# Groups of two row units instead of four in batches 2 to 6 of a masked graph layer with LayerNorm, with a new start and a new end

## The chip, the cores and the metric
One core of one Trainium2 chip. The metric is the device time of one launch in microseconds (us). The kernel before takes 120.64 us, the median of 3 runs (120.59 to 120.68). PE is TensorE (PEld its weight loads), DVE is VectorE, ACT is ScalarE, POOL is GpSimd, SP is SyncE, which issues the transfers.

## The reference
Eight batches, 1024 nodes of 128 features, four relations with a 128x128 weight each. adj holds 0 or 1 for these inputs, of type int32, so only the mask of relation 1 has ones.

```python
x, adj        # (8, 1024, 128) float32; (8, 1024, 1024) int32
masks = (adj[None] == rel_ids[:, None, None, None]).astype(x.dtype)
h = jnp.einsum('rbnm,bmd->rbnd', masks, x)
y = jnp.einsum('rbnd,rdo->bno', h, weight) + bias
out = layernorm(x + y, axis=-1)            # eps 1e-5
```

## The kernel before, in words
A batch has 1024 rows in eight **units** of 128 rows. Relation 1 alone is computed; meanwhile the kernel checks that adj holds 0 and 1 only and that x is in range, and a second pass for all relations runs if not (here it doesn't).

For each unit:
- SP loads adj, 0.5 MiB a unit; from batch 1's second pair on, two units (a pair, 1 MiB) at a time (`load_adj`, L398). Three slots of a batch each, a ring: a load waits until the pair three batches back is transposed and checked.
- PE transposes the low half-words of the unit, eight 128x128 blocks (`transpose_unit`, L601), into one of four PSUM banks `ids_t`.
- DVE makes bf16 0/1 values of them in `mask_t` (`mask_unit`, L699).
- ACT checks a pair with a squaring activation (`check`, L522).

For each batch, x is split into a float16 high part `x_hi` (ACT, `split_hi`, L531) and the rest `x_lo` (POOL, `split_lo`, L448; DVE in batch 0). POOL then adds the bias to x in place (`add_bias`, L454), for the residual sum.

Rows go on in **groups** of units (`split`, L70): four units in batches 2 to 6, in batch 1 two, in batch 0 one or two, in batch 7 four, two, one, one. For each group PE makes 16 matmuls, eight with x_hi and eight with x_lo, with up to 512 moving columns (`products`, L619), ACT copies the result to SBUF (`copy_h`, L535), PE multiplies it with the weight, one fp32 matmul a unit, into `y_ps` (`project`, L633), DVE adds x plus bias (`sum_rows`, L705), and makes statistics (L711) and moments (L717). For each batch ACT takes a square root (`root`, L539), DVE a reciprocal (`offer_guess`, L727), POOL refines it in seven small operations (`roots`, L465 to L481) and normalises the rows (L488). SP stores them after all loads.

**Order.** Each engine's program is written out by hand. PE's step for group g (L661 to L668) is: for each unit of the next group, transpose it, then do that share of g's products; the projection of group g-1 stands before the last share. So a group of two is: transpose, half the products, transpose, projection of g-1, half the products. `project(g)` for a group before the last four waits for the sum of group g-1 (L631), since both use `y_ps`.

DVE's step for g (L796 to L817): the sum of g-2, masks of the next group's units with the statistics of g-2, the row maxima of x_hi (in a batch's first group) and, where g-2 ends a batch, moments and the reciprocal between them.

ACT's step for g (L558 to L568): copy_h of g-1; where g is the last group of its batch, split_hi of the next batch; then the checks that `pairs_checked_by` gives to g, and after the first of them the root of a batch that g-2 ended.

POOL's order (L494 to L499) is, for each b: split_lo(b+1), roots(b-1), normalise(b-1), add_bias(b+1). `split_lo` waits for `s_hi`, and `sum_rows` (L704) for `s_xb`, which `add_bias` counts up:

```python
for b in range(B - 1):
    split_lo(b + 1)
    if b >= 1:
        roots(sets[b - 1])
        normalise(sets[b - 1], sets[b - 1].units)
    add_bias(b + 1)
```

SP's order: units of batch 0 with the weight behind unit 1, unit (1,0), x(1), unit (1,1), three pairs of batch 1, x(2), then for each batch from 2 its four pairs and the next batch's x. x(0) is loaded whole from ACT's queue. A batch is read with rows p*8+s in batches 0 and 1 and in blocks of two rows (`step`) later.

At the end, batch 7 is normalised in two sets of four units, the first (`ra`) on POOL and ACT, the second (`rb`) with a chain of five small DVE operations after its root.

Of the kernel before, what the change touches and what calls it, by code (L numbers as in the profile page):

```python
# [5 lines left out]
P = 128  # L6
FP32 = mybir.dt.float32
# [4 lines left out]
ALU = mybir.AluOpType  # L12
# [27 lines left out]
def adj_resnorm_kernel(nc, x, adj, weight, bias, out):  # L40
# [14 lines left out]
    def step(b):  # L55
        return J if b < EARLY else 2

# [12 lines left out]
    def split(b):  # L70
        if b == 0:
            return [(0, 1), (1, 1), (2, 2), (4, 2), (6, 2)]
        if b == 1:
            return [(0, 2), (2, 2), (4, 2), (6, 2)]
        return [(0, 4), (4, 2), (6, 1), (7, 1)] if b == B - 1 else [(0, 4), (4, 4)]

# [33 lines left out]
    def pairs_checked_by(g):  # L110

        first = [1, 2, 2, 3, 4, 5, 6, 7, 8, 11, 13]
        if g.index < len(first):
            return first[g.index]
        return min(PAIRS * (g.b + 1) + (2 if ends_batch(g) else 0), PAIRS * B)

    ctx = ExitStack()
    with ctx:
# [8 lines left out]

        ident = sb("ident", [P, P], BF16)
        ones = sb("ones", [P, 1], FP32)
        row_of_ones = sb("row_of_ones", [1, P], FP32)  # L130
# [53 lines left out]
        s_biased = sem("bias_ready")  # L184
        s_unit = [[sem(f"unit_loaded{b}{u}") if alone(b, u) else None for u in range(J)] for b in range(EARLY)]
        s_x = [sem(f"x_loaded{b}") for b in range(B)]
        s_adj = [[sem(f"adj_loaded{slot}{k}") for k in range(PAIRS)] for slot in range(ADJ_SLOTS)]
# [3 lines left out]
        s_zero = sem("ident_zeroed")  # L191
        s_ident = sem("ident_ready")
        s_const = sem("constants_ready")
        s_still = sem("zeros_ready")
# [196 lines left out]
        def _(sp):  # L391
# [17 lines left out]

            load_unit(0, 0)  # L410
            load_unit(0, 1)
            sp.dma_start(w_sb[:, 0, :], weight[0]).then_inc(s_w, 16)  # L412
            for u in range(2, J):
                load_unit(0, u)
            load_unit(1, 0)
            load_x(1)
            load_unit(1, 1)
            for k in range(1, PAIRS):
                load_adj(1, k)
            load_x(2)  # L420
            for b in range(EARLY, B):
                for k in range(PAIRS):
                    load_adj(b, k)
                if b + 1 < B:
                    load_x(b + 1)

# [11 lines left out]
        def _(pool):  # L438
            nc.gpsimd.memset(ident[:, :], 0.0).then_inc(s_zero, 1)
            pool.wait_ge(s_zero, 1)  # L440
            nc.gpsimd.affine_select(out=ident[:, :], in_=ident[:, :], compare_op=ALU.not_equal, fill=1.0,
                                    base=0, pattern=[[-1, P]], channel_multiplier=1).then_inc(s_ident, 1)

            def split_lo(b):
# [56 lines left out]
            roots(full)  # L501
            normalise(full, full.units[:4])
            roots(ra)
# [5 lines left out]
        def _(act):  # L509
# [15 lines left out]

            def split_hi(b, js, signal):
                act.wait_ge(s_x[b], 16)
                if b >= 2:
                    act.wait_ge(s_prod, last_group_of(b - 2) + 1)
                    act.wait_ge(s_rm, b - 1)  # L530
                nc.scalar.activation(x_hi[:, b % 2, js], x_sb[:, b, js], ACT.Copy).then_inc(signal, 1)  # L531
# [16 lines left out]

            act.dma_start(units_of(x_sb[:, 0], 0, 0, J), rows_of(x, 0, 0, J)).then_inc(s_x[0], 16)
            act.dma_start(bias_row[:, :], bias.rearrange("(a d) -> a d", a=1)).then_inc(s_bias, 16)  # L550
            act.preload_act_table(ACT.Sqrt)
            split_hi(0, slice(0, HALF), s_hi0)
            split_hi(0, slice(HALF, J), s_hi)
            act.wait_ge(s_spread, 1)
# [3 lines left out]
            for g in groups[1:LAST]:  # L558
                b = g.b
                copy_h(groups[g.index - 1])  # L560
                if ends_batch(g):
                    split_hi(b + 1, slice(0, J), s_hi)
                todo = range(pairs_checked_by(groups[g.index - 1]), pairs_checked_by(g))
                for n, at in enumerate(todo):
                    check(at // PAIRS, at % PAIRS)
                    q = groups[g.index - 2] if g.index >= 2 else None
                    if n == 0 and q and ends_batch(q):
                        root(sets[q.b])  # L568
            a, c, e, d = groups[LAST:]
# [6 lines left out]
            copy_h(c)  # L576
            normalise(full, full.units[4:5])
            copy_h(e)
            root(ra)
            normalise(full, full.units[5:7])  # L580
            copy_h(d)
            normalise(full, full.units[7:]).then_inc(s_aside, 1)
            root(rb)
# [5 lines left out]
        def _(pe):  # L589
# [35 lines left out]
            def project(g):  # L625
# [6 lines left out]
                for n in range(g.count):  # L632
                    last = nc.tensor.matmul(y_of(g)[:, n, :], h_all[:, g.bank, n * P:(n + 1) * P], w_sb[:, 0, :],  # L633
                                            start=True, stop=True)
                last.then_inc(s_y, 1)

            def idle_turns(n):
# [4 lines left out]
            pe.wait_ge(s_still, 1)  # L642
            idle_turns(9)
            pe.wait_ge(s_ident, 1)
# [8 lines left out]
            transpose_unit(0, 1)  # L653
            products(g, 1, 2)
            g = groups[1]
            products(g, 0, 2)
            transpose_unit(0, 2)
            project(groups[0])
            products(g, 1, 2)
            transpose_unit(0, 3)  # L660
            for g in groups[2:LAST + 1]:  # L661
                coming = coming_after(g)
                for n, u in enumerate(coming):
                    transpose_unit(groups[g.index + 1].b, u)

                    if n == (len(coming) - 1 if g.index < LAST else 1):
# [8 lines left out]
            products(d, 0, 1)  # L675
            project(e)
            pe.wait_ge(s_found, 1)
            nc.tensor.matmul(ids_t[0][0:1, 0, 0:2].bitcast(FP32), found[:, :], ones[:, :],
                             start=True, stop=True).then_inc(s_count, 1)
            project(d)  # L680
            second_pass(pe, second_pe)

        @block.vector
        def _(dve):
# [23 lines left out]
            def statistics(g):  # L708
                dve.wait_ge(s_sum, g.index + 1)
                for u in g.units:  # L710
                    last = nc.vector.bn_stats(stats[:, u, :], rows[:, g.b, u, :])  # L711
                last.then_inc(s_st, 1)

            def combine(r, g, units):
# [38 lines left out]

            def normalise(r, units):
                wait_for_rstd(dve, r)
                slot = r.b
                for u in units:
                    last = nc.vector.tensor_scalar(rows[:, slot, u, :], rows[:, slot, u, :], mean[:, slot, u:u + 1],  # L758
                                                   rstd[:, slot, u:u + 1], ALU.subtract, ALU.mult)
                last.then_inc(s_done, 1)  # L760

# [79 lines left out]
            combine(rb, c, c.units)  # L841
            for g in (e, d):
                sum_rows(g)
                statistics(g)
            combine(rb, d, range(J - 2, J))
            dve.wait_ge(s_count, 1)
            nc.vector.tensor_copy(again[:, :], ids_t[0][0:1, 0, 0:2].bitcast(FP32)).then_inc(s_again, 1)
            for part in (invert, times_guess, times_guess_again, better_guess, shift_rows):
                part(rb)
            normalise(rb, rb.units[2:])  # L850
            second_pass(dve, second_dve)
# [17 lines left out]
```

## Time and profile before
| | |
|---|---|
| median of 3 runs | 120.64 us |
| the profiled execution | 120.54 us |
| its span | 118.8 us |
| PE busy | 106.6 us, 90% |
| DVE, ACT, POOL busy | 84.8 (71%), 88.1 (74%), 70.3 us (59%) |
| transfers | 42.22 MB, mean 355 GB/s |
| granted clock of PE | 0.985 |

The span is the time from the first to the last instruction in the trace; the execution's own time is 1.74 us longer. Times in rows are counted from the start of the span. The timeline's rows give start, length, engine, line, operation, tiles and count, and in brackets how long the engine was idle before and what ended that. Runs of equal instructions are merged into a row, and its length ends with the last of them; matmuls overlap, so the distance of two starts says more than a length.

### The profile page before, as it was taken

To read this page: it belongs to the slowest core of one execution; us is meant where nothing else is said; L and a number is where in the kernel's file an instruction comes from. 1 tells how busy PE (TensorE), PEld (TensorE's weight loads), DVE (VectorE), ACT (ScalarE), POOL (GpSimd) and SP (SyncE) were. 2 spreads that over 40 slices of the span, in tenths; PEclk is the share of its full clock that TensorE was granted. 3 is DMA by queue.
4 is the path that set the end of the run, shared out by engine and by line. 5 is a ranking of instruction groups with operands and counts; after the bars stand their busy time and mean duration, and the time that the engine had idled before them with its cause. 6 is when DMAs were issued, how large, how long until landed. Compare 5 with 4: busy or idle time off the path is not lost.

```text
span 118.8 us, 2879 instructions
## 1 busy us (share of the span) xinstructions
PE 106.6 (90%) x1012; PEld 80.4 (68%) x1023; DVE 84.8 (71%) x252; ACT 88.1 (74%) x114; POOL 70.3 (59%) x132
## 2 busy tenths in 40 slices
PE   6788999899999979999999999999999999999400
PEld 2168898799997646767676767676868676679300
DVE  1055678397877848696959887787779777998840
ACT  4088277947797999799999499968987698925530
POOL 2007001940047998399569955995689577977740
PEclk9999999999999999999999999999999999999985
DMA  3999999999999999999999999999999999450271
GB/s 73 389 408 411 414 407 422 414 391 412 425 414 384 419 403 436 380 414 414 419 391 404 422 406 394 420 406 423 377 433 411 415 399 383 141 177 0 85 248 35
DMA packets 12419, 42.22 MB, mean 355 GB/s; under 512 B 882, under 2 KB 7155, under 8 KB 8947
## 3 DMA queue, kind: packets, MB, share of 16 engines
q1 hardware_dynamic: 12256, 41.49, 88.6%
q10 hardware_dynamic: 146, 0.52, 1.3%
q8 instruction: 9, 0.15, 0.5%
q14 instruction: 8, 0.06, 0.1%
HBM read 37.81 MB, written 4.19 MB: 354 GB/s over the span
## 4 chain that ended last, share of the span: by engine, by line
PE 58%; DMA 29%; SPq 5%; DVE 2%; issue 1%; ACT 0%; DVEq 0%
PE h_ps L619 32%; DMA adj_sb<-adj 29%; PE ids_t L601 16%; PE y_ps L633 9%; SPq L396 4%; PE ids_t L633 1%; DVE x_sb L758 0%; SPq L393 0%; SPq L412 0%; ACT std L539 0%; DVE stats L711 0%; DVE x_sb L705 0%; DVE moments L717 0%; DVEq L255 0%; DVE shift L751 0%
## 5 line engine op out<-in xcount | busy, mean ns | idle before, releaser
L522 ACT ACTIVATE junk<-adj_sb,minus 128x2048 bf16<-128x2048 int32 x32 | 63.8, 1994 | 0.4 <-DMA adj_sb<-adj 0.4
L699 DVE TENSOR_SCALAR mask_t<-ids_t 128x1024 bf16<-128x1024 uint16 x64 | 43.6, 687 | 25.2 <-PE ids_t L601 24.1
L601 PEld LDWEIGHTS ids_t<-ident,adj_sb 128*128 128x128 bf16 x512 | 36.5, 123 | 13.8 <-DMA adj_sb<-adj 2.7
L601 PE MATMUL ids_t<-ident,adj_sb 128*128 128x128 bf16 x512 | 40.0, 221 | 2.3 <-DMA adj_sb<-adj 2.2
L619 PE MATMUL h_ps<-mask_t,x_lo 128*128 128x512 bf16 (+2 forms) x184 | 33.5, 314 | 0.0
L619 PE MATMUL h_ps<-mask_t,x_hi 128*128 128x512 bf16 (+2 forms) x173 | 31.1, 310 | 1.2 <-DVE mask_t L699 0.6
L448 POOL TENSOR_TENSOR x_lo<-x_sb,x_hi 128x1024 f16<-128x1024 f32 x7 | 15.0, 2144 | 24.2 <-ACT x_hi L531 24.2
L488 POOL TENSOR_SCALAR x_sb<-x_sb,rstd,shift 128x128 f32<-128x128 f32 x55 | 24.0, 457 | 1.0
L535 ACT ACTIVATE h_all<-h_ps 128x512 f32<-128x512 f32 (+2 forms) x23 | 10.6, 463 | 18.1 <-PE h_ps L619 18.1
L454 POOL TENSOR_TENSOR x_sb<-x_sb,bias_sb 128x1024 f32<-128x1024 f32 x8 | 19.0, 2377 | 7.8 <-DVE x_lo L764 7.7
L619 PEld LDWEIGHTS h_ps<-mask_t,x_hi 128*128 128x128 f16 x184 | 15.6, 98 | 7.2 <-DVE mask_t L699 1.2
L619 PEld LDWEIGHTS h_ps<-mask_t,x_lo 128*128 128x128 f16 x184 | 16.4, 98 | 5.9
L633 PE MATMUL y_ps<-w_sb,h_all 128*128 128x128 f32 x120 | 17.8, 284 | 0.0
L633 PEld LDWEIGHTS y_ps<-w_sb,h_all 128*128 128x128 f32 x120 | 15.0, 192 | 0.1
L711 DVE BATCH_NORM_STATS2 stats<-x_sb 128x6 f32<-128x128 f32 x64 | 14.5, 280 | 0.1
L705 DVE TENSOR_TENSOR x_sb<-y_ps,x_sb 128x512 f32<-128x512 f32 (+2 forms) x20 | 11.0, 552 | 1.9 <-PE y_ps L633 1.0
L531 ACT ACTIVATE x_hi<-x_sb 128x1024 f16<-128x1024 f32 (+1 forms) x9 | 8.5, 954 | 3.1 <-DMA x_sb<-x 3.1
L692 DVE TENSOR_REDUCE row_max<-x_hi 128x8 f32<-128x1024 f16 x8 | 9.6, 1202 | 0.0
L522 ACT ACTIVATION_READ_ACCUMULATOR junk<-adj_sb,minus 128x1 f32 x32 | 6.1, 190 | 0.0
L640 PE MATMUL h_ps<-mask_t 128*128 128x512 bf16 x11 | 4.6, 586 | 1.2 <-DVE mask_t L787 1.2
L717 DVE BATCH_NORM_AGGREGATE moments<-stats 128x2 f32<-128x6 f32 x64 | 5.3, 154 | 0.1
L470 POOL TENSOR_TENSOR product<-sixteenth,first_guess 128x8 f32<-128x8 f32 (+1 forms) x8 | 1.6, 203 | 6.2 <-DVE first_guess L727 6.0
(44 smaller groups left out, 30.8 us busy)
## 6 DMA issues: line engine op xcount, KB each, us to landing
adj_sb<-adj SPq DMA_DIRECT2D x27, 1024.0 KB, 19.5
adj_sb<-adj SPq DMA_DIRECT2D x10, 512.0 KB, 8.4
x_sb<-x SPq DMA_DIRECT2D x7, 512.0 KB, 18.9
out<-x_sb SPq DMA_DIRECT2D x7, 512.0 KB, 16.7
x_sb<-x ACTq DMA_DIRECT2D x1, 512.0 KB, 5.4
out<-x_sb SPq DMA_DIRECT2D x2, 256.0 KB, 3.3
w_sb<-weight SPq DMA_DIRECT2D x1, 64.0 KB, 6.1
bias_row<-bias ACTq DMA_DIRECT2D x1, 0.5 KB
```

What stands on the lines that cost most here:

```text
L448: nc.gpsimd.tensor_tensor(x_lo[:, b % 2], x_sb[:, b], x_hi[:, b % 2], ALU.subtract).then_inc(s_lo, 1)
L454: nc.gpsimd.tensor_tensor(x_sb[:, b], x_sb[:, b], bias_sb[:, :].unsqueeze(1).to_broadcast([P, J, D]), ALU.add).then_inc(s_xb, 1)
L488: last = nc.gpsimd.tensor_scalar(rows[:, slot, u, :], rows[:, slot, u, :], rstd[:, slot, u:u + 1], shift[:, slot, u:u + 1], ALU.mult, ALU.add)
L522: nc.scalar.activation(junk[:, at % 2], adj_sb[:, slot, 2 * k:2 * k + 2, :], ACT.Square, scale=2.0, bias=minus[:, 0:1], accum_out=squares[ ...
L535: nc.scalar.activation(h_all[:, g.bank, 0:g.count * P], h_ps[g.bank][:, 0:g.count * P], ACT.Copy).then_inc(s_h, 1)
L601: last = nc.tensor.transpose(bank[:, j, :], words[:, j // step(b), j % step(b), 0, :], ident[:, :])
L619: last = nc.tensor.matmul(h_ps[g.bank][:, 0:g.count * P], part[:, g.b % 2, j, :], mask_t[:, g.b % 2, j, g.cols], start=(j == 0 and part is ...
L633: last = nc.tensor.matmul(y_of(g)[:, n, :], h_all[:, g.bank, n * P:(n + 1) * P], w_sb[:, 0, :], start=True, stop=True)
L692: nc.vector.tensor_reduce(row_max[:, b, :], x_hi[:, b % 2], AX.X, ALU.max, apply_absolute_value=True).then_inc(s_rm, 1)
L699: nc.vector.tensor_scalar(mask_t[:, b % 2, :, u * P:(u + 1) * P], ids_t[u % T_BANKS][:, :, :].bitcast(UINT16), 1.0, None, ALU.mult).then_i ...
L705: nc.vector.tensor_tensor(rows[:, g.b, g.us, :], y_of(g)[:, 0:g.count, :], x_sb[:, g.b, g.us, :], ALU.add).then_inc(s_sum, 1)
L711: last = nc.vector.bn_stats(stats[:, u, :], rows[:, g.b, u, :])
```

## The change
- `split`: batches 2 to 6 in groups of two units, as batch 1 already; `step` is 2 in batch 1 too.
- x(0) is loaded in halves on SP behind unit (0,0); each half has a semaphore for its split. x(1) goes behind unit (1,1), and from batch 2 on x(b) behind the second pair of its own batch.
- In batch 0, PE transposes units 2 and 3 a step earlier; one idle matmul less ahead.
- ACT does split_hi(b+1) after the first check of the step instead of ahead of the checks; `pairs_checked_by` spreads the checks one or two to a group.
- The last unit (group d): PE adds x into y with an fp32 identity (`add_x`), DVE takes statistics and normalises from PSUM, no sum_rows; the count's matmul goes behind. ACT's and POOL's shares of batch 6's normalisation are 2 units on POOL and 6 on ACT instead of 4 and 4.

```diff
-        return J if b < EARLY else 2
+        return J if b == 0 else 2
...
-        if b == 1:
-            return [(0, 2), (2, 2), (4, 2), (6, 2)]
-        return [(0, 4), (4, 2), (6, 1), (7, 1)] if b == B - 1 else [(0, 4), (4, 4)]
+        return [(0, 4), (4, 2), (6, 1), (7, 1)] if b == B - 1 else [(0, 2), (2, 2), (4, 2), (6, 2)]
...
-        first = [1, 2, 2, 3, 4, 5, 6, 7, 8, 11, 13]
+        first = [1, 2, 2, 3, 4, 5, 6, 7, 8, 10, 11]
...
-        return min(PAIRS * (g.b + 1) + (2 if ends_batch(g) else 0), PAIRS * B)
+        return min(PAIRS * g.b + g.place + (2 if g.b < 4 else 3), PAIRS * B) if g.b < B - 1 else PAIRS * B
...
             load_unit(0, 0)
+            for n in range(2):
+                sp.dma_start(x_sb[:, 0, n * HALF:(n + 1) * HALF, :], rows_of(x, 0, n * HALF, HALF)).then_inc(s_x0[n], 16)
             load_unit(0, 1)
...
             load_unit(1, 0)
+            load_unit(1, 1)
             load_x(1)
-            load_unit(1, 1)
             for k in range(1, PAIRS):
                 load_adj(1, k)
-            load_x(2)
-            for b in range(EARLY, B):
+
+            for b in range(2, B):
                 for k in range(PAIRS):
                     load_adj(b, k)
-                if b + 1 < B:
-                    load_x(b + 1)
+                    if k == 1:
+                        load_x(b)
...
+            pool.wait_ge(s_ident, 1)
+            nc.gpsimd.tensor_copy(whole_ident[:, :], ident[:, :]).then_inc(s_whole, 1)
...
-            normalise(full, full.units[:4])
+            normalise(full, full.units[:2])
...
                 copy_h(groups[g.index - 1])
-                if ends_batch(g):
-                    split_hi(b + 1, slice(0, J), s_hi)
                 todo = range(pairs_checked_by(groups[g.index - 1]), pairs_checked_by(g))
                 for n, at in enumerate(todo):
                     check(at // PAIRS, at % PAIRS)
-                    q = groups[g.index - 2] if g.index >= 2 else None
-                    if n == 0 and q and ends_batch(q):
-                        root(sets[q.b])
+                    if n == 0:
+                        q = groups[g.index - 2] if g.index >= 2 else None
+                        if q and ends_batch(q):
+                            root(sets[q.b])
+                        if ends_batch(g):
+                            split_hi(b + 1, slice(0, J), s_x[b + 1], s_hi)
...
-            normalise(full, full.units[4:5])
+            normalise(full, full.units[2:3])
             copy_h(e)
             root(ra)
-            normalise(full, full.units[5:7])
+            normalise(full, full.units[3:5])
             copy_h(d)
-            normalise(full, full.units[7:]).then_inc(s_aside, 1)
+            normalise(full, full.units[5:]).then_inc(s_aside, 1)
...
+            def add_x(g):
+
+                pe.wait_ge(s_whole, 1)
+                pe.wait_ge(s_xb, g.b + 1)
+                nc.tensor.matmul(y_of(g)[:, 0, :], whole_ident[:, :], x_sb[:, g.b, g.first, :], start=True, stop=False)
...
-            idle_turns(9)
+            idle_turns(8)
...
             products(g, 1, 2)
+            transpose_unit(0, 2)
             g = groups[1]
             products(g, 0, 2)
-            transpose_unit(0, 2)
+            transpose_unit(0, 3)
             project(groups[0])
             products(g, 1, 2)
-            transpose_unit(0, 3)
...
             project(e)
+            add_x(d)
+            project(d)
...
-            project(d)
...
-            for g in (e, d):
-                sum_rows(g)
-                statistics(g)
+            sum_rows(e)
+            statistics(e)
+            statistics_of_sum(d)
```

## Rows read from the trace of the kernel before

**Rows 1.** The page, engine busy time, share of the span, instructions
```profile
PE 106.6 (90%) x1012; PEld 80.4 (68%) x1023; DVE 84.8 (71%) x252; ACT 88.1 (74%) x114; POOL 70.3 (59%) x132
```

**Rows 2.** Windows, one batch: stretch, length, busy of PE, PEld, DVE, ACT, POOL, clock, DMA share, GB/s
```profile
55.68:68.05 12.37, 12.27 (x111) 8.70 (x112) 9.96 (x29) 10.77 (x14) 9.43 (x18) 1.00 1.03 410
```

**Rows 3.** Timeline, transposes on PE that waited for a load of adj
```profile
6.42 0.70 PE L601 MATMUL ids_t<-ident,adj_sb 128*128 128x128 bf16 x8 [1.21 <-DMA adj_sb<-adj]
...
22.84 0.73 PE L601 MATMUL ids_t<-ident,adj_sb 128*128 128x128 bf16 x8 [0.42 <-DMA adj_sb<-adj]
...
43.30 0.64 PE L601 MATMUL ids_t<-ident,adj_sb 128*128 128x128 bf16 x8 [0.58 <-DMA adj_sb<-adj]
```

**Rows 4.** Timeline, PE, batch 3: a group of four between its first transposes
```profile
49.52 0.61 PE L601 MATMUL ids_t<-ident,adj_sb 128*128 128x128 bf16 x8
...
54.84 1.03 PE L619 MATMUL h_ps<-mask_t,x_lo 128*128 128x512 bf16 x4
...
55.71 0.61 PE L601 MATMUL ids_t<-ident,adj_sb 128*128 128x128 bf16 x8
```

**Rows 5.** Timeline, PE, batch 1: groups of two
```profile
26.15 0.67 PE L601 MATMUL ids_t<-ident,adj_sb 128*128 128x128 bf16 x8
...
27.53 0.66 PE L601 MATMUL ids_t<-ident,adj_sb 128*128 128x128 bf16 x8
...
28.03 0.66 PE L633 MATMUL y_ps<-w_sb,h_all 128*128 128x128 f32 x4
...
28.53 1.04 PE L619 MATMUL h_ps<-mask_t,x_lo 128*128 128x256 bf16 x8
...
29.41 0.67 PE L601 MATMUL ids_t<-ident,adj_sb 128*128 128x128 bf16 x8
...
32.65 0.61 PE L601 MATMUL ids_t<-ident,adj_sb 128*128 128x128 bf16 x8
```

**Rows 6.** Timeline, POOL and DVE: a sum of two units, add_bias(3), and batch 3's first sum
```profile
26.32 0.42 DVE L705 TENSOR_TENSOR x_sb<-y_ps,x_sb 128x256 f32<-128x256 f32 x1
...
53.77 2.37 POOL L454 TENSOR_TENSOR x_sb<-x_sb,bias_sb 128x1024 f32<-128x1024 f32 x1
...
61.23 0.69 DVE L705 TENSOR_TENSOR x_sb<-y_ps,x_sb 128x512 f32<-128x512 f32 x1
```

**Rows 7.** Timeline, ACT, the last step of batch 1 and a check after it
```profile
32.85 0.38 ACT L535 ACTIVATE h_all<-h_ps 128x256 f32<-128x256 f32 x1 [0.79 <-PE h_ps L619]
...
33.13 1.05 ACT L531 ACTIVATE x_hi<-x_sb 128x1024 f16<-128x1024 f32 x1
...
37.17 1.99 ACT L522 ACTIVATE junk<-adj_sb,minus 128x2048 bf16<-128x2048 int32 x1
```

**Rows 8.** Timeline, POOL: split_lo(2), the first of roots(0), normalise(0), add_bias(2)
```profile
34.26 2.14 POOL L448 TENSOR_TENSOR x_lo<-x_sb,x_hi 128x1024 f16<-128x1024 f32 x1 [9.30 <-ACT x_hi L531]
36.49 0.20 POOL L465 TENSOR_SCALAR sixteenth<-moments 128x8 f32<-128x8 f32 x1
...
38.60 3.47 POOL L488 TENSOR_SCALAR x_sb<-x_sb,rstd,shift 128x128 f32<-128x128 f32 x8
42.02 2.38 POOL L454 TENSOR_TENSOR x_sb<-x_sb,bias_sb 128x1024 f32<-128x1024 f32 x1
```

**Rows 9.** Timeline, the end: PE's long step of batch 7, sum of its first group, last root
```profile
99.01 0.61 PE L601 MATMUL ids_t<-ident,adj_sb 128*128 128x128 bf16 x8
...
107.25 0.69 DVE L705 TENSOR_TENSOR x_sb<-y_ps,x_sb 128x512 f32<-128x512 f32 x1
...
112.20 0.30 ACT L539 ACTIVATE std<-moments,eps 128x4 f32<-128x4 f32 x1 [1.14 <-DVE moments L717]
```

**Rows 10.** Windows after the last matmul, columns as in rows 2
```profile
114.20:114.80 0.60, 0.00 (x0) 0.00 (x0) 0.02 (x1) 0.00 (x0) 0.00 (x0) 1.00 0.60 201
114.80:115.40 0.60, 0.00 (x0) 0.00 (x0) 0.00 (x0) 0.00 (x0) 0.00 (x0) 0.77 0.98 309
```

More of the change, by code:

```diff
@@ L128, in adj_resnorm_kernel @@
         ident = sb("ident", [P, P], BF16)
+        whole_ident = sb("whole_ident", [P, P], FP32)
         ones = sb("ones", [P, 1], FP32)
@@ L185, in adj_resnorm_kernel @@
         s_unit = [[sem(f"unit_loaded{b}{u}") if alone(b, u) else None for u in range(J)] for b in range(EARLY)]
+        s_x0 = [sem(f"half_of_first_x_loaded{n}") for n in range(2)]
         s_x = [sem(f"x_loaded{b}") for b in range(B)]
@@ L192, in adj_resnorm_kernel @@
         s_ident = sem("ident_ready")
+        s_whole = sem("whole_ident_ready")
         s_const = sem("constants_ready")
@@ L524, in check, with split_hi @@
                                      accum_out=squares[:, at:at + 1]).then_inc(s_check, 1)
-            def split_hi(b, js, signal):
-                act.wait_ge(s_x[b], 16)
+            def split_hi(b, js, loaded, signal):
+                act.wait_ge(loaded, 16)
                 if b >= 2:
@@ L547, in normalise @@
                 return last
-            act.dma_start(units_of(x_sb[:, 0], 0, 0, J), rows_of(x, 0, 0, J)).then_inc(s_x[0], 16)
             act.dma_start(bias_row[:, :], bias.rearrange("(a d) -> a d", a=1)).then_inc(s_bias, 16)
             act.preload_act_table(ACT.Sqrt)
-            split_hi(0, slice(0, HALF), s_hi0)
-            split_hi(0, slice(HALF, J), s_hi)
+            split_hi(0, slice(0, HALF), s_x0[0], s_hi0)
+            split_hi(0, slice(HALF, J), s_x0[1], s_hi)
             act.wait_ge(s_spread, 1)
@@ L633, in project @@
                     last = nc.tensor.matmul(y_of(g)[:, n, :], h_all[:, g.bank, n * P:(n + 1) * P], w_sb[:, 0, :],
-                                            start=True, stop=True)
+                                            start=g.index < len(groups) - 1, stop=True)
                 last.then_inc(s_y, 1)
+            def add_x(g):
+                pe.wait_ge(s_whole, 1)
+                pe.wait_ge(s_xb, g.b + 1)
+                nc.tensor.matmul(y_of(g)[:, 0, :], whole_ident[:, :], x_sb[:, g.b, g.first, :], start=True, stop=False)
             def idle_turns(n):
@@ L712, in statistics, with statistics_of_sum @@
                 last.then_inc(s_st, 1)
+            def statistics_of_sum(g):
+                dve.wait_ge(s_y, g.index + 1)
+                nc.vector.bn_stats(stats[:, g.first, :], y_of(g)[:, 0, :]).then_inc(s_st, 1)
             def combine(r, g, units):
@@ L752, in shift_rows, with normalise @@
                                                in1=rstd[:, r.b, r.us], op0=ALU.mult, op1=ALU.mult).then_inc(s_rstd_last, 1)
-            def normalise(r, units):
+            def normalise(r, u, source):
                 wait_for_rstd(dve, r)
[L756 to L760, printed above, removed]
+                return nc.vector.tensor_scalar(rows[:, r.b, u, :], source, mean[:, r.b, u:u + 1], rstd[:, r.b, u:u + 1],
+                                               ALU.subtract, ALU.mult)
             def split_lo(b, js, hi, lo):
@@ L849, in _ @@
                 part(rb)
-            normalise(rb, rb.units[2:])
+            normalise(rb, e.first, rows[:, rb.b, e.first, :])
+            normalise(rb, d.first, y_of(d)[:, 0, :]).then_inc(s_done, 1)
             second_pass(dve, second_dve)
```

## The prediction, made before the change was run
> **What bounds the kernel now.** I read the page's busy shares first: TensorE is busy 106.6 of 118.8 us [rows 1]. A share can hide stages, so the windows came next: a whole batch in the middle takes 12.37 us and TensorE is busy 12.27 of it, at granted clock 1.00, while VectorE has 9.96, ScalarE 10.77, GpSimd 9.43 [rows 2]. The transfers move 410 GB/s there, so one MiB takes 2.56 us and a batch's 4.5 MiB 11.5 us: close behind, but not the bound. The chain of waits in order of time shows where that was otherwise: TensorE waited for a pair of adj at 22.84 and at 43.30, and before its first transpose at 6.42 [rows 3]; from 43.30 to 111.24 it has no gap. The two waits lie 8 MiB of queue apart (7 MiB up to pair (1,1), 15 up to pair (3,0)): 8 x 2.56 = 20.5 us, as observed. So there are two clocks: the transfers until 43, TensorE afterwards.
>
> **The start.** The first x no longer shares the start with unit 0, so unit 0 has 0.5 MiB less in front of it: first transpose 1.28 us earlier, near 5.1 instead of 6.42 [rows 3]. Transposing a unit ahead takes away mask waits of 0.3 us or so. But pair (1,1) stands behind the same 7 MiB as before, so TensorE only waits longer at 22.84: I count 0. The two half loads and the later ones are issued on SP 0.4 us apiece, faster than they move; bounds of the start: 1.3 gained, 0.5 lost. x(1), now behind unit (1,1), lands 1 MiB before pair (1,1), at 22.84 - 2.56 = 20.3; the products want its split half a microsecond after 22.84. From batch 2 on, x comes after the second pair: x(2) lands 3.5 MiB ahead of the old place of (3,0), at 43.3 - 9.0 = 34.3, and its split starts at 35.1 (below): no cost. It is also moved past the slot waits of two pairs on SP, which end a batch or more before need. The fp32 identity is one small GpSimd copy in its idle time at the start: 0. One idle matmul fewer: 0.
>
> **Groups of two: TensorE.** A group of four takes 49.52 to 55.71 = 6.19 us [rows 4]. Batch 1 already has groups of two: 26.15, 29.41, 32.65, so 3.25 each, 6.50 for four units [rows 5]. The products themselves cost the same: four of 512 columns 0.87 (54.84 to 55.71), eight of 256 columns 0.88 (28.53 to 29.41). What is added is one more switch between transposes, products and projection for every four units. That is 0.31 us per four units, 0.62 per batch, 3.1 us for the five batches 2 to 6. The Trainium skill (TensorE: Matmul & The Clock Gate, LDWEIGHTS) prices a weight load at its columns over 1.2 GHz, 107 ns for 128, and twice as many loads are issued; by it a matmul of 256 columns is only just covered. The rows agree that it is still covered, at 110 ns each.
>
> **Groups of two: the wait that appears.** Three edits meet. (a) split_hi(b+1) stands in the last step of batch b, which was half a batch (6.19 us) and is now a quarter (3.25), and it now stands behind a check of 1.99 us. (b) GpSimd's order is unchanged: split_lo(b+1), roots(b-1), normalise(b-1), add_bias(b+1). (c) sum_rows of the first group of batch b needs add_bias(b). It comes two steps later: that was the start of the next batch, and is now the middle of the same one. Before, add_bias(3) was over at 53.77 + 2.37 = 56.14 and sum_rows wanted it at 61.23: 5.1 us of slack [rows 6]. Now, from the start c of the last step of a batch:
> - ScalarE: copy_h starts at c + 0.20 (32.65 to 32.85), 0.28 to the next instruction, the check 1.99, split_hi 1.05 [rows 5, 7]: c + 3.52.
> - GpSimd: 0.08 handover, then split_lo at 34.26 to the end of add_bias at 42.02 + 2.38 = 44.40, 10.14 us without a gap [rows 8]: c + 13.74.
> - VectorE: handover 0.05 (an estimate from the 0.08 just shown), sum_rows of two units 0.42 [rows 6]: c + 14.21. Here project of the second group waits, since it may not write y_ps before this sum.
> - TensorE: handover and first weight load 0.12, project 0.50, half the products 0.87: c + 15.7. That is the last step of the next batch, which starts the ring again.
>
> So a batch takes **15.7 us**, and not 4 x 3.25 = 13.0: TensorE is ready for that projection two and a half steps into the batch and a bit, at c + 3 x 3.25 + 0.50 + 0.88 + 0.45 = 11.6, so it stands for 2.6 us. (x_lo is ready at c + 5.75, where TensorE wants it at c + 3.25 + 2.3 = 5.55: a wait of 0.2 that this stall swallows.) VectorE's masks are queued behind the waiting sum_rows: two masks (0.69 each) and 0.48 of statistics after it end at c + 16.1, when the first half products of the last step want them: just in time. Nothing else is late, for VectorE's 9.96 and ScalarE's 10.77 us per batch [rows 2] grow by under 1 us each (two more sums of 0.42 and two more copies, for halves of the old ones), in a batch of 15.7, and GpSimd has 10.1. No engine is full; it is a ring of dependences.
>
> **The sum.** The last step of batch 1 starts at 32.65 as before. Five turns of the ring (add_bias 2 to 6): 32.65 + 5 x 15.7 = 111.15. That step now transposes four units for batch 7, two more than 3.25 us hold: 4.1 us, so batch 7's own long step begins at 115.25. It began at 99.01 [rows 9]: **+16.24**. In batch 7 add_bias(7) ends 13.74 - 4.1 = 9.64 after that start, and sum_rows of its first group wanted it after 107.25 - 99.01 = 8.24. The root of batch 6 follows it on GpSimd (2.1 us, 36.49 to 38.60), so shift(6) comes at 11.7 instead of 9.6. ScalarE's copy of group e is queued behind a normalise that waits for it: 0.49, then copy 0.26, root 0.30, two units 0.86, copy 0.27, three units 1.3, so root(rb) starts at 15.3 instead of 112.20 - 99.01 = 13.19: **+2.1**. The sum for the last unit moves to TensorE (a matmul of 0.25 instead of 0.30 on VectorE), hidden behind this. Everything after root(rb), stores included, is 6.6 us as before; the three last stores come closer together, 0 to 0.3. Span 118.8 + 16.24 + 2.1 = 137.1; the profiled execution lies 1.74 above its span: 138.9. It is 120.54 against a median of 120.64, so add 0.1: **139.0 us**, 15% slower.
>
> Unknown: the five turns at 0.15 each way (0.8), the tail between 0 and 3, the start -1.3 to +0.5, handovers under load. Together 135.6 to 141.8.
>
> **Rivals.**
> 1. The ring does not close: add_bias is early enough, and TensorE alone sets the time. For it: no engine is full, and no stall of this sort is in the trace. Against it: GpSimd's order and 10.14 us [rows 8] against a need at c + 11.6. Then 120.6 + 3.1, less 0.3 in the tail: 123.4. Chance 0.05.
> 2. The stalls lower TensorE's clock. After its last matmul at 111.24 the clock is still 1.00 through 114.80 and falls after it [rows 10], so 3.56 us of idleness were granted and mine are 2.5. It decides from a stall above that; with the next step (3.25 us of work) at half rate each time, 5 x 3.25 = 16 us more: 155. The Trainium skill (TensorE: Matmul & The Clock Gate, The HAM clock gate) states that 1.2 GHz is the idle state and that activity releases 2.4. The rows agree in kind and let this stall pass. Chance 0.04.
> 3. The other side, faster: the first transpose near 5.1 carries through because pair (1,1) lands earlier too, once x does not run on a second queue beside it. This needs the wait of 0.42 at 22.84 [rows 3] not to grow, and both the ring and the 3.1 us of rows 5 to be absent. It gives 120.6 - 1.3 - 0.3 = 119.0. It decides if a two-unit step in mid kernel takes 3.1 and not 3.25 us. Chance 0.03.
>
> **How the numbers follow.** The ring has 0.88, and its range 135.6 to 141.8 holds nine tenths of that: 8 in 10, so the range need not reach the rivals. About 0.2% is what a measurement tells from no change. Faster 0.03 (rival 3), same 0.01 (rivals 1 and 3 blended), slower 0.96.
>
> **What would show it.** In the profile after: the distance between two add_bias instructions in batches 3 to 6 is 15.7 us, GpSimd idle 5.5 us in each, ahead of split_lo; TensorE idle about 2.5 us before a projection in the third step of each batch; VectorE's sum_rows ended by "POOL x_sb L454"-like waits, once per batch; the clock stays 1.00; the wait at 22.84 has grown to about 1.5 us. It is wrong if GpSimd's spacing is 13, if the stall sits before split_lo or a mask, or if the clock drops.

## The result and the profile after

| | before | after |
|---|---|---|
| median | 120.66 us (4 runs) | 142.58 us (4 runs: 141.88, 142.45, 142.71, 144.2) |
| ratio of the times, 95% interval | | 1.181 (1.175 to 1.187) |
| the profiled execution, its span | 120.54, 118.8 us | 141.88, 140.1 us |
| PE busy | 106.6 us, 90% | 114.1 us, 81% |
| granted clock of PE | 0.985 | 0.948 |

The change costs 22 us. The forecast was 139.0, with a range up to 141.8: right in sign and in most of its size (18 of 22 us), and too low. The profiled execution is the fastest of the four. The ratios, here and below, leave out executions more than 1.5% above the fastest of the same kernel: the one of 144.2 us here, one each in E1, E4 and E5, two in E9, and one of 623.75 us of the kernel before beside E1 to E4, which stays unexplained.

The page of the changed kernel, busy time and the chain that ended last:

```profile
PE 114.1 (81%) x1183; PEld 100.1 (71%) x1184; DVE 87.7 (63%) x261; ACT 89.7 (64%) x126; POOL 69.8 (50%) x131
...
POOL 45%; issue 33%; PE 6%; DMA 5%; ACT 4%; SPq 2%; DVE 1%; DVEq 0%; POOLq 0%
```

Against [rows 1] the other engines have about the work they had, and all have a smaller share of a longer span. TensorE shows 7.5 us more. E3 below does the same work without stalls and has 107.9 us, so some 6 us of these are matmuls at a lower clock. The chain now runs through GpSimd, which is busy half the time. That is what a ring of waits looks like: the chain is on an engine with no lack of time.

The waits of the changed kernel (who waited for whom; us in total, times, longest):

```profile
POOL x_lo L453 <- ACT x_hi L536: 52.8, 7, 12.1
...
DVE x_sb L717 <- POOL x_sb L459: 15.2, 5, 3.4
...
PE y_ps L638 <- DVE x_sb L717: 11.9, 5, 2.7
...
PE h_ps L624 <- POOL x_lo L453: 0.6, 3, 0.2
```

Five times, once for each of batches 2 to 6, sum_rows waits for add_bias and a projection for sum_rows. Neither wait was in the trace before. The other wait foreseen, for x_lo, is 0.2 us.

GpSimd's timeline: split_lo and add_bias of batches 2 to 7, in brackets its idle time before:

```profile
37.06 2.15 POOL L453 TENSOR_TENSOR x_lo<-x_sb,x_hi 128x1024 f16<-128x1024 f32 x1 [9.81 <-ACT x_hi L536]
44.85 2.35 POOL L459 TENSOR_TENSOR x_sb<-x_sb,bias_sb 128x1024 f32<-128x1024 f32 x1
52.85 2.15 POOL L453 TENSOR_TENSOR x_lo<-x_sb,x_hi 128x1024 f16<-128x1024 f32 x1 [5.66 <-ACT x_hi L536]
60.62 2.34 POOL L459 TENSOR_TENSOR x_sb<-x_sb,bias_sb 128x1024 f32<-128x1024 f32 x1
69.46 2.15 POOL L453 TENSOR_TENSOR x_lo<-x_sb,x_hi 128x1024 f16<-128x1024 f32 x1 [6.50 <-ACT x_hi L536]
...
85.69 2.14 POOL L453 TENSOR_TENSOR x_lo<-x_sb,x_hi 128x1024 f16<-128x1024 f32 x1 [6.10 <-ACT x_hi L536]
...
101.47 2.15 POOL L453 TENSOR_TENSOR x_lo<-x_sb,x_hi 128x1024 f16<-128x1024 f32 x1 [5.66 <-ACT x_hi L536]
...
118.59 2.15 POOL L453 TENSOR_TENSOR x_lo<-x_sb,x_hi 128x1024 f16<-128x1024 f32 x1 [7.01 <-ACT x_hi L536]
```

From one split_lo to the next: 15.79, 16.61, 16.23, 15.78 and 17.12 us. Two turns are the 15.7 of the forecast within 0.1; three are 0.5 to 1.4 longer. GpSimd's own part, split_lo to the end of add_bias, is 52.85 to 62.96 = 10.11 us, as in [rows 8].

One turn as TensorE and VectorE have it, from the stall of batch 3 on:

```profile
63.06 0.42 DVE L717 TENSOR_TENSOR x_sb<-y_ps,x_sb 128x256 f32<-128x256 f32 x1 [3.33 <-POOL x_sb L459]
...
63.63 0.69 PE L638 MATMUL y_ps<-w_sb,h_all 128*128 128x128 f32 x4 [2.62 <-DVE x_sb L717]
...
64.15 1.88 PE L624 MATMUL h_ps<-mask_t,x_lo 128*128 128x256 bf16 x8
...
65.83 1.06 PE L606 MATMUL ids_t<-ident,adj_sb 128*128 128x128 bf16 x8
...
80.27 0.68 PE L638 MATMUL y_ps<-w_sb,h_all 128*128 128x128 f32 x4 [2.22 <-DVE x_sb L717]
...
82.06 1.06 PE L606 MATMUL ids_t<-ident,adj_sb 128*128 128x128 bf16 x8
...
96.48 0.68 PE L638 MATMUL y_ps<-w_sb,h_all 128*128 128x128 f32 x4 [1.81 <-DVE x_sb L717]
...
112.26 1.20 PE L638 MATMUL y_ps<-w_sb,h_all 128*128 128x128 f32 x4 [2.63 <-DVE x_sb L717]
...
114.95 0.82 PE L606 MATMUL ids_t<-ident,adj_sb 128*128 128x128 bf16 x8
```

(the projections at 80.27, 96.48 and 112.26 are those after the stalls of batches 4, 5 and 6; the transposes at 65.83, 82.06 and 114.95 begin the batch's last step), and the windows over two such stalls, at 46 and at 62 us (stretch, length, busy of PE, PEld, DVE, ACT, POOL, granted clock, DMA share, GB/s):

```profile
46.00:47.00 1.00, 0.00 (x0) 0.00 (x0) 0.00 (x0) 0.00 (x0) 1.00 (x1) 1.00 1.04 421
...
47.80:48.80 1.00, 0.93 (x8) 0.92 (x9) 1.00 (x4) 0.00 (x0) 0.00 (x0) 1.00 1.02 426
...
62.40:63.60 1.20, 0.00 (x0) 0.00 (x0) 0.54 (x2) 0.00 (x0) 0.56 (x1) 1.00 1.00 416
...
64.20:65.00 0.80, 0.80 (x7) 0.55 (x5) 0.80 (x4) 0.00 (x0) 0.00 (x0) 0.50 1.11 461
...
67.00:68.00 1.00, 1.00 (x8) 0.78 (x7) 1.00 (x3) 1.00 (x1) 0.00 (x0) 0.71 1.18 415
```

After the stall at 46 (idle for 2.66 us) the clock stays at 1.00. After that at 62 (idle for 2.62) it is at 0.50, 1.2 instead of 2.4 GHz, from about 64.2 to 67.4. It falls again after the third and the fifth stall. The half of the group's products between the projection and the next last step takes 65.83 - 64.15 = 1.68 us instead of 0.87.

### The profile page after: what moved, and what is told of

The parts are those of the page before. It is cut to its first block, busy times and chain, and to the rows that moved or that the text cites. A ratio compares the mean times of both kernels' runs of the same rounds, so it can differ in the third digit from the quotient of the medians.

```text
span 140.1 us, 3262 instructions
## 1 busy us (share of the span) xinstructions
PE 114.1 (81%) x1183; PEld 100.1 (71%) x1184; DVE 87.7 (63%) x261; ACT 89.7 (64%) x126; POOL 69.8 (50%) x131
## 4 chain that ended last, share of the span: by engine, by line
POOL 45%; issue 33%; PE 6%; DMA 5%; ACT 4%; SPq 2%; DVE 1%; DVEq 0%; POOLq 0%
POOL x_sb L493 15%; POOL x_sb L459 12%; POOL x_lo L453 11%; DMA adj_sb<-adj 5%; PE h_ps L624 3%; PE ids_t L606 2%; ACT junk L527 1%; POOL product L481 1%; POOL minus_mean L472 1%; POOL better L478 1%; POOL rstd L483 1%; POOL product L475 1%; SPq L397 1%; POOL shift L486 1%; POOL sixteenth L470 1%
## 5 line engine op out<-in xcount | busy, mean ns | idle before, releaser
L606 PE MATMUL ids_t<-ident,adj_sb 128*128 128x128 bf16 x512 | 41.2, 225 | 3.5 <-DMA adj_sb<-adj 3.4
L624 PE MATMUL h_ps<-mask_t,x_lo 128*128 128x256 bf16 (+2 forms) x264 | 35.9, 280 | 0.6 <-POOL x_lo L453 0.6
L624 PE MATMUL h_ps<-mask_t,x_hi 128*128 128x256 bf16 (+2 forms) x263 | 34.8, 276 | 0.1
L540 ACT ACTIVATE h_all<-h_ps 128x256 f32<-128x256 f32 (+2 forms) x33 | 12.2, 369 | 33.8 <-PE h_ps L624 33.8
L638 PE MATMUL y_ps<-w_sb,h_all 128*128 128x128 f32 x120 | 20.6, 295 | 11.9 <-DVE x_sb L717 11.9
L624 PEld LDWEIGHTS h_ps<-mask_t,x_lo 128*128 128x128 f16 x264 | 25.3, 102 | 4.6 <-POOL x_lo L453 1.2
L624 PEld LDWEIGHTS h_ps<-mask_t,x_hi 128*128 128x128 f16 x264 | 24.2, 101 | 3.4 <-DVE mask_t L711 0.3
L638 PEld LDWEIGHTS y_ps<-w_sb,h_all 128*128 128x128 f32 x120 | 16.2, 196 | 12.7 <-issue 12.6
L493 POOL TENSOR_SCALAR x_sb<-x_sb,rstd,shift 128x128 f32<-128x128 f32 x53 | 23.2, 454 | 1.2 <-DVE shift L768 0.4
L717 DVE TENSOR_TENSOR x_sb<-y_ps,x_sb 128x256 f32<-128x256 f32 (+2 forms) x30 | 12.5, 416 | 15.2 <-POOL x_sb L459 15.2
L550 ACT ACTIVATE x_sb<-x_sb,shift,rstd 128x128 f32<-128x128 f32 x9 | 4.0, 485 | 2.8 <-POOL shift L486 2.6
```

The source lines that it names most:

```text
L493: last = nc.gpsimd.tensor_scalar(rows[:, slot, u, :], rows[:, slot, u, :], rstd[:, slot, u:u + 1], shift[:, slot, u:u + 1], ALU.mult, ALU.add)
L540: nc.scalar.activation(h_all[:, g.bank, 0:g.count * P], h_ps[g.bank][:, 0:g.count * P], ACT.Copy).then_inc(s_h, 1)
L606: last = nc.tensor.transpose(bank[:, j, :], words[:, j // step(b), j % step(b), 0, :], ident[:, :])
L624: last = nc.tensor.matmul(h_ps[g.bank][:, 0:g.count * P], part[:, g.b % 2, j, :], mask_t[:, g.b % 2, j, g.cols], start=(j == 0 and part is ...
L717: nc.vector.tensor_tensor(rows[:, g.b, g.us, :], y_of(g)[:, 0:g.count, :], x_sb[:, g.b, g.us, :], ALU.add).then_inc(s_sum, 1)
```

## The experiments

Eleven kernels ran, each beside the kernel before on its own chip; the ratios are to that. E1 to E4 shared one chip, E5 to E8 another, E9 to E11 a third.

### E1 to E3: is it the ring?

E1 moves add_bias, E2 moves split_hi, E3 does both.

```diff
                 split_lo(b + 1)
+                add_bias(b + 1)
                 if b >= 1:
                     roots(sets[b - 1])
                     normalise(sets[b - 1], sets[b - 1].units)
-                add_bias(b + 1)
```

```diff
                 copy_h(groups[g.index - 1])
+                if ends_batch(g):
+                    split_hi(b + 1, slice(0, J), s_x[b + 1], s_hi)
...
-                        if ends_batch(g):
-                            split_hi(b + 1, slice(0, J), s_x[b + 1], s_hi)
```

> The changed kernel, but GpSimd does add_bias(b+1) directly behind split_lo(b+1), ahead of roots and normalise. Ring theory (the wait for add_bias makes the stall and so the time): the stall before the projection in the third step disappears in all five batches, add_bias ends 8.1 us after the last step's start where 11.6 is wanted, the distance between two split_lo falls from 15.8 to 17.1 down to about 13.0 us (x_lo may still be 0.4 late), the clock stays 1.00, time 125 to 126.5 us. Rival, that groups of two cost this by themselves (VectorE's masks or the handovers on TensorE): time stays over 138.

> The changed kernel, but split_hi(b+1) stands ahead of the check again. Ring theory: the ring is shorter by exactly the check, 1.99 us, so 13.8 us between two add_bias, stall 0.6 to 1.1 us a batch, too short for the clock to fall: 129 to 130 us. Rival, that the place of split_hi does not matter since ScalarE has spare time: 142 as the changed kernel.

> Both edits: add_bias behind split_lo, split_hi ahead of the check. Ring theory: no ring and no wait for x_lo left, TensorE alone, 4 x 3.14 = 12.56 us a batch, 121 to 122.5 us, about 1 us slower than the kernel before. If something else of groups of two binds (VectorE's row maxima before a mask, copies on ScalarE), the batch takes longer than 12.6 and the windows show which engine TensorE waits for.

| | median us | ratio (interval) | expected |
|---|---|---|---|
| E1 | 125.54 | 1.040 (1.035 to 1.045) | 125 to 126.5 |
| E2 | 129.01 | 1.070 (1.066 to 1.074) | 129 to 130 |
| E3 | 122.80 | 1.018 (1.013 to 1.023) | 121 to 122.5 |

GpSimd of E1, two split_lo in a row, and TensorE's wait between:

```profile
63.19 2.14 POOL L453 TENSOR_TENSOR x_lo<-x_sb,x_hi 128x1024 f16<-128x1024 f32 x1 [2.75 <-ACT x_hi L536]
...
76.14 2.14 POOL L453 TENSOR_TENSOR x_lo<-x_sb,x_hi 128x1024 f16<-128x1024 f32 x1 [2.75 <-ACT x_hi L536]
```

```profile
65.38 1.05 PE L624 MATMUL h_ps<-mask_t,x_lo 128*128 128x256 bf16 x8 [0.20 <-POOL x_lo L453]
```

E2, the same, with the stall that is left:

```profile
63.66 2.15 POOL L453 TENSOR_TENSOR x_lo<-x_sb,x_hi 128x1024 f16<-128x1024 f32 x1 [3.67 <-ACT x_hi L536]
...
77.44 2.15 POOL L453 TENSOR_TENSOR x_lo<-x_sb,x_hi 128x1024 f16<-128x1024 f32 x1 [3.67 <-ACT x_hi L536]
```

```profile
74.44 0.68 PE L638 MATMUL y_ps<-w_sb,h_all 128*128 128x128 f32 x4 [0.96 <-DVE x_sb L717]
```

A batch takes 12.95 us in E1 and 13.78 in E2. The undisturbed turn was 15.79, and the check that E2 takes out of the ring is 1.99 long: 15.79 - 1.99 = 13.80. So the ring has the members and the length that the forecast gave it. The order of two instructions on GpSimd, whose total work is the same, is worth 17 us of the change's 22 (142.58 to 125.54), the falls of the clock among them. E3 leaves no wait on TensorE inside batches 3 to 6; its batches take 12.6 us, and it is 0.3 us above its bracket. Two waits for ScalarE's copies are left in batch 2 (0.31 and 0.89 us).

### E4: the clock

```diff
                 elif g.index <= LAST:
+                    if g.place == 1 and 2 <= g.b < B - 1:
+                        for _ in range(40):
+                            nc.tensor.matmul(spare, ident[:, :], ident[:, :], start=True, stop=True)
                     pe.wait_ge(s_sum, g.index)
```

> The changed kernel with 40 unneeded matmuls of 128 columns (2.2 us) on TensorE in front of the wait for sum_rows, in the third step of batches 2 to 6; they compute nothing that is used. Clock theory (three of the five stalls let the clock fall to half, and this costs the turns their 0.9, 0.5 and 1.4 us over 15.7): all five turns take 15.7 to 15.8 us, clock 1.00 throughout, time 138.8 to 139.4. Rival, that the longer turns have another cause: turns still 16.2 to 17.1, time 141.9 or more.

139.36 us, ratio 1.150 (1.143 to 1.156); the stall in which TensorE idles shrinks to 0.3 us, and the clock is 1.00 in every window of 2 us from 2 to 132 us. One of the five stalls, and its split_lo:

```profile
63.57 0.71 PE L642 MATMUL y_ps<-w_sb,h_all 128*128 128x128 f32 x4 [0.28 <-DVE x_sb L721]
```

```profile
52.91 2.14 POOL L454 TENSOR_TENSOR x_lo<-x_sb,x_hi 128x1024 f16<-128x1024 f32 x1 [5.59 <-ACT x_hi L537]
...
68.59 2.14 POOL L454 TENSOR_TENSOR x_lo<-x_sb,x_hi 128x1024 f16<-128x1024 f32 x1 [5.60 <-ACT x_hi L537]
...
84.26 2.15 POOL L454 TENSOR_TENSOR x_lo<-x_sb,x_hi 128x1024 f16<-128x1024 f32 x1 [5.60 <-ACT x_hi L537]
```

Each of the five turns is 15.7 us now (15.71, 15.68, 15.67, 15.68, 15.69). Work that nobody uses, put into the stall, makes the kernel 3.2 us faster. So the longer turns were the clock's doing, and without them the kernel takes 139.4, the forecast's 139.0 within 0.4. The turns are right by their mechanism; that the total comes so close is also luck, for the start is late by about as much as the end is short (0.8 and 1.0 us in the changed kernel, in the sum further down).

### E5 and E6: the late start

Both are E3 with x(0) in one piece, E5 on ScalarE's queue as in the kernel before, E6 on SP's queue.

E6:

```diff
-            for n in range(2):
-                sp.dma_start(x_sb[:, 0, n * HALF:(n + 1) * HALF, :], rows_of(x, 0, n * HALF, HALF)).then_inc(s_x0[n], 16)
+            load_x(0)
```

E5 has the first line's loop taken out and instead, ahead of the bias on ScalarE's queue:

```diff
+            act.dma_start(units_of(x_sb[:, 0], 0, 0, J), rows_of(x, 0, 0, J)).then_inc(s_x[0], 16)
```

> The kernel with both edits (add_bias behind split_lo, split_hi ahead of the check) and x(0) loaded whole on ScalarE's queue as in the kernel before, not in halves on SP. In the changed kernel the transfers run at some 330 GB/s from 3.5 to 8 us where the kernel before has 410, and pair (1,1) arrives at 24.02 and not 22.84. Theory A (one queue alone, or the halves, slow the start): pair (1,1) is back near 22.8, and the time falls by 0.8 to 1.2 us against the run with both edits (122.8), to 121.6 to 122.0. Rival B (the lateness has to do with x(1), the rows' layout of batch 1 or chance): no change, 122.8.

> As the last, but x(0) whole on SP's queue behind unit (0,0): rows of 4 KB a partition instead of two transfers of 2 KB rows. If the size of the halves is what slows the start, pair (1,1) is back near 22.8 and the time is that of x on ScalarE's queue, 121.6 to 122.0. If it is the single queue, pair (1,1) still arrives near 24 and the time stays 122.8.

E5 122.28 us, 1.011 (1.007 to 1.015), 0.3 above what theory A gave it; E6 123.04 us, 1.019 (1.016 to 1.022), near the 122.8 that was expected if the single queue is the cause. The rates say one thing and the times another. GB/s of the stretches 4 to 5, 5 to 6, 6 to 8 us, from the windows:

| x(0) | run | GB/s |
|---|---|---|
| halves on SP | changed kernel | 328, 324, 346 |
| halves on SP | E3 | 326, 356, 384 |
| whole on SP | E6 | 426, 422, 404 |
| whole on ScalarE's | E5 | 410, 418, 412 |

The halves slow the transfers of the first 8 us, and not the queue: E6 has the changed kernel's queue and the full rate. But pair (1,1) comes at 23.70 in E3, 23.00 in E6 and 24.06 in E5 (from an execution of 123.58 us, well above its median), and the times do not follow the rates. E6 has the full rate and is no faster than E3 (1.019 against 1.018). E5 differs from E6 only by the queue and is 0.8 us faster, with intervals that do not touch. By the times it would be the queue, by the rates the halves, and these runs do not settle it. Over all thirteen traces pair (1,1) comes at 23.5 to 24.2 with the halves (six runs), at 23.0 to 24.1 with x(0) whole and batch 1 in blocks of two rows (E5, E6, E8, E9), and at 22.8 to 23.2 with x(0) whole and rows p*8+s (the kernel before, E10, E11). So the halves are not the only part of the change that goes with a later pair; the layout of batch 1 is another.

### E7 to E9: the rest of the change, with groups of four

E7 is the changed kernel with the groups and checks as before; E8 has x(0) whole on ScalarE's queue too; E9 also has split_hi ahead of the check (the diff of E2) and nine idle matmuls.

```diff
-        return [(0, 4), (4, 2), (6, 1), (7, 1)] if b == B - 1 else [(0, 2), (2, 2), (4, 2), (6, 2)]
+        if b == 1:
+            return [(0, 2), (2, 2), (4, 2), (6, 2)]
+        return [(0, 4), (4, 2), (6, 1), (7, 1)] if b == B - 1 else [(0, 4), (4, 4)]
```

> The changed kernel with groups of four in batches 2 to 6 and the checks spread as in the kernel before; start, order of the loads, end and the place of split_hi behind the check are those of the change. Ring theory: the ring has over 4 us of slack with groups of four, so no stall before a projection and no fall of the clock; TensorE is late by up to 0.9 us at 43 because the transfers start late, and gains 0.3 at the end: 120.0 to 121.3. Rival, that the other edits (split_hi behind a check, start, end) carry a good part of the loss by themselves: over 123.

> As the last, with x(0) whole on ScalarE's queue. If theory A holds, the start is no longer late, and what is left of the change is a gain: 119.4 to 120.4, below the kernel before (120.7). If B holds, equal to the last.

> Groups of four, x(0) whole on ScalarE's queue, split_hi ahead of the check, nine idle matmuls again; the rest as the change has it. In e8 root(rb) starts 13.57 us after the long step of batch 7 begins, and 13.19 in the kernel before, since GpSimd's work begins a check later and shift(6) with it. If that is what eats the new end, it falls to 12.9 or less and the time to 119.9 to 120.5, 0.5 below e8 and faster than the kernel before. If the new end is worth nothing by itself, it stays at e8's 121.0.

E7 121.55 us, 1.008 (1.005 to 1.011); E8 121.03, 1.002 (0.999 to 1.005); E9 120.81, 0.999 (0.996 to 1.002). So everything in the change but the groups costs about 1 us together, with the same late split_hi: the slack of four units swallows it. E7 lies 0.25 above its bracket, E8 0.6 and E9 0.3. E9 was expected 0.5 below E8 and is 0.2 below in the median, well within the intervals. It is not shown that its edits make the kernel faster. E7 and E8 have the new wait of the end, ScalarE's normalise for shift(6). E7's ACT:

```profile
109.87 0.49 ACT L552 ACTIVATE x_sb<-x_sb,shift,rstd 128x128 f32<-128x128 f32 x1 [1.15 <-POOL shift L488]
```

and behind it the copy of group e, for which TensorE then waits. In the kernel before this wait was 0.17 us, and in E9 it is 0.16.

### E10 and E11: batch 1's row layout

E10 is E5, and E11 is E9, with one line undone:

```diff
-        return J if b == 0 else 2
+        return J if b < EARLY else 2
```

> e5 (groups of two, both edits, x(0) whole on ScalarE's queue) with the row layout of batch 1 as in the kernel before (rows p*8+s instead of blocks of two rows). Theory C: a transpose whose stationary operand is read with a stride of 32 bytes takes longer than one with 8, eight transposes 0.50 us and not 0.45, so the steps of batch 1 go from 3.14 back to 3.25 us; and x(1) in rows of 1 KB is what makes the transfers dip to 370 GB/s from 14 to 18 us, so the dip goes. Time within 0.4 of e5 (122.3), since the two offset. If the steps stay at 3.14, the layout has no part in it.

> e9 with batch 1's row layout as in the kernel before. By theory C 0.1 us a step lost in batch 1, hidden in the wait for transfers at 37 to 43 us, and the dip at 14 to 18 us gone: equal to e9 within 0.4.

E10 122.50 us, 1.013 (1.009 to 1.017), as expected. E11 **120.39 us, 0.9955 (0.9936 to 0.9974)**: the one version whose interval lies below the kernel before, by half a per cent. It still holds several edits of the change, and no run separates which of them gives this. Batch 1's steps on TensorE in the changed kernel and in E10:

```profile
27.18 0.61 PE L606 MATMUL ids_t<-ident,adj_sb 128*128 128x128 bf16 x8
...
30.32 0.61 PE L606 MATMUL ids_t<-ident,adj_sb 128*128 128x128 bf16 x8
```

```profile
26.46 0.67 PE L605 MATMUL ids_t<-ident,adj_sb 128*128 128x128 bf16 x8
...
29.71 0.67 PE L605 MATMUL ids_t<-ident,adj_sb 128*128 128x128 bf16 x8
```

3.14 us with blocks of two rows, 3.25 with rows p*8+s. The steps bear out theory C, and so do the rates: the transfers from 14 to 18 us run at 369, 372 and 382 GB/s in E5, E6 and E8, and at 415 in E10 and 410 in E11. The changed kernel itself, whose start was slow already, has 408 there, so this part is shown for the runs with x(0) in one piece alone. E11's median is 0.4 below E9's on the same chip, at the edge of what was expected, and their intervals overlap.

E11 also shows what the new end can give. Its long step of batch 7 and its last root:

```profile
98.49 0.61 PE L607 MATMUL ids_t<-ident,adj_sb 128*128 128x128 bf16 x8
...
111.36 0.30 ACT L544 ACTIVATE std<-moments,eps 128x4 f32<-128x4 f32 x1
```

12.87 us apart, the 12.9 expected of E9 (which has 12.86), against 13.57 in E8 and 13.19 in [rows 9]. With split_hi early, GpSimd reaches shift(6) early, and the end is 0.3 us shorter; with split_hi late, it is 0.4 longer.

## Where the prediction was right, and where it fell short

By its own steps, for the profiled execution:

- **The bound before, the cost of 256 columns, the ring.** Right, and by the mechanism that was forecast: GpSimd idle 5.66 to 7.01 us ahead of split_lo, TensorE idle 1.81 to 2.66 us before the projection in each third step. From c = 49.26 the split_lo starts at c + 3.59 (3.60 forecast), add_bias ends at c + 13.70 (13.74), and sum_rows at 63.48, c + 14.22 (14.21). E1, E2 and E4 took the ring apart term by term.
- **"So 3.56 us of idleness were granted and mine are 2.5", rival 2 at 0.04.** This step failed, and it is why the time left the range: "the clock stays 1.00" was counted on, and a clock that drops was among the forecast's own signs of being wrong. It took one stretch of idleness, at the end of the kernel before, for a bound that stalls elsewhere must reach. Stalls of 2.62, 2.22 and 2.63 us were followed by a clock of 1.2 GHz, those of 2.66 and 1.81 were not. It also priced the fall as a whole step at half rate each time, 16 us. Only what is on the ring counts: the projection and half the products. In turn two 65.83 - 64.15 = 1.68 us instead of 0.87, hence 0.8; in turn three (80.27 to 82.06) 1.79 instead of 1.39, hence 0.4; in turn five (112.26 to 114.95) 2.69 instead of 1.39, hence 1.3. Together 2.5 of the 3.0 us by which the five turns, 81.5 us, exceed 78.5; the rest is 0.1 us a turn. It was a part of the forecast's own case and not a rival to it: here the falls came behind the ring's stalls. The fall varies from run to run: the four runs have a mean clock of 0.948 (141.88 us), 0.924 (142.45), 0.926 (142.71) and 0.919 (144.2). Only the first has a trace, so that the other three are longer for the same reason is likely and not shown.
- **"I count 0" for the start.** The first transpose came at 5.09, as forecast (5.1). Pair (1,1) came at 24.02 and not 22.84: 1.2 us lost where the bound was 0.5. In the first 10 us the transfers moved 266 GB/s in the mean instead of 304, 0.38 MB less, which at 410 GB/s is 0.9 of the 1.2 us. The step set x(0)'s 0.5 MiB as bytes in a queue and took the rate for the same whatever the size of the rows.
- **Groups of two at 3.25 us, 3.1 us in all.** Oversized. The 3.25 was read from batch 1, whose layout the change alters too; the new step takes 3.14, so with no ring the cost is 12.6 - 12.38 = 0.2 us a batch. The step blamed one more switch for all of the 0.31 us per four units; 0.22 of it was the row layout, and 0.09 is left for the switch. [rows 5] show it already: eight transposes of batch 1 take 0.67 us, those at 32.65, which are of batch 2, 0.61. In the ring the term has no weight, and in batch 1 the new layout gave 0.4 us back before the ring begins. It is also the sign that rival 3 named, a step of 3.1 us, and rival 3 did not hold: the ring was there and the wait for pair (1,1) grew.
- **The tail.** root(rb) came 14.58 us after the long step's start (133.77 - 119.19), not 15.3: ScalarE's instructions start some 0.1 us before the record of the one in front ends, five times, and the terms as listed add up to 15.2. The stores took 0.3 less.
- **The range.** The bounds that the forecast lists (0.8 each way, the tail 0 to 3, the start -1.3 to +0.5) add up to 134.8 to 141.2 and not to 135.6 to 141.8; what the handovers may add has no number there.

Sum: 137.1 of span, + 0.8 start with batch 1, + 3.0 turns, + 0.1 last step, - 0.7 and - 0.3 at the end = 140.0, against 140.1. In it + 0.9 and - 1.0 cancel: the start and the end were each wrong by about 1 us.

The windows at 62 to 68 us above show the clock at 1.00 in the stall, at 0.50 behind it and back at 1.00 after some 3 us of work. The rule of the Trainium skill weighed in rival 2 (TensorE: Matmul & The Clock Gate, The HAM clock gate), that an idle array drops to 1.2 GHz and activity releases it, agrees with them in kind. It does not say which of two equal stalls here is followed by the fall.

## What to carry to other kernels

Before making groups smaller, list every engine's hand-written order and ask how many groups lie between producer and consumer: a distance counted in groups shrinks with them, and an engine at 50% busy can then set the period. A ring shows itself as a chain through an idle engine, equal distances, and a period that shrinks by exactly what is moved out of it. If stalls of about 2 us or more on TensorE cannot be avoided, budget for a lower clock behind some of them (three of five here, each costing 0.4 to 1.3 us); unneeded matmuls in the stall bought 3 us here.

## What was not expected of the hardware

- Eight transposes whose stationary operand is read with a stride of 32 bytes take 0.50 us, with 8 bytes 0.45 us (batch 1 in E10 and in the changed kernel: 3.25 against 3.14 us a step of 16 transposes).
- Loading x(0) in two halves, with 2 KB a partition and row, instead of once with 4 KB lowered the rate between 4 and 6 us from 410 to 426 GB/s to 324 to 356 (table of E5 and E6); with x(0) whole, 1 KB rows in x(1) gave 369 to 382 instead of 410 to 415 GB/s between 14 and 18 us (E5, E6, E8 against E10, E11). In the six runs with halves the same rows of x(1) show a smaller dip or none (394 to 408). x in later batches has 1 KB rows too, in the kernel before as well, and there the rate is 410 [rows 2]; why it shows in batch 1 alone stays open.
- Equal stalls of 2.6 us do not always have the same effect on the clock. Waits for transfers did it too: in E5, E8 and E9 the clock was at 0.50 for some 3 us behind waits of 2.07 and 1.89 us for the first unit and of 2.60 us for pair (1,1), and the changed kernel's wait of 1.63 us for that pair left it at 1.00. In E5 and E8 the slower stretch, at 7 to 12 us, ends ahead of a later wait for pair (1,1), so by the trace it costs nothing.
